# Moving GpSimd's second k*v of a pass to the end of the pass before, and the third of the first pass up to VectorE's bonus

## What is computed

```python
xn = _ln(x, ln1_w, ln1_b)
sx = _token_shift(xn, state[:, i1])
xxx = tanh((xn + sx * maa_x) @ maa_w1) ... @ maa_w2
x5 = xn[:, :, None] + sx[:, :, None] * (maa_stack + xxx)
w = exp(-exp(time_decay + tanh(x5[:, :, 1] @ decay_w1) @ decay_w2))
r, k, v = x5[:, :, 3] @ Wr.T, x5[:, :, 0] @ Wk.T, x5[:, :, 2] @ Wv.T
g = silu(x5[:, :, 4] @ Wg.T)
def step(s, rkvw):
    a = k_t[:, :, :, None] * v_t[:, :, None, :]
    out = einsum('bhk,bhkd->bhd', r_t, u * a + s)
    return (a + w_t[:, :, :, None] * s, out)
...
x = x + (group_norm(att) * g) @ Wo.T
...
x = x + rr * (kk @ ffn_Wv.T)
```

## Time and profile before

| | us |
|---|---|
| median of three runs | 703.38 (702.08 to 706.02) |
| the profiled execution | 699.89 |
| its span in the profile | 698.0 |
| TensorE busy | 623.4 (89%) |
| VectorE busy | 595.5 (85%) |
| ScalarE busy | 390.9 (56%) |
| GpSimd busy | 294.3 (42%) |

### The profile page before, as it was taken

How to read it: one execution, slowest core, us unless ns; L and a number is a source line. 1 busy time by engine, 2 the same in 40 slices (tenths; PEclk the granted TensorE clock), 3 DMA queues, 4 the chain that set the end, 5 groups by cost and what they waited for, 6 DMA issues and landing times.

```text
span 698.0 us, 9609 instructions
## 1 busy us (share of the span) xinstructions
PE 623.4 (89%) x2694; PEld 335.1 (48%) x2694; DVE 595.5 (85%) x902; ACT 390.9 (56%) x933; POOL 294.3 (42%) x210
## 2 busy tenths in 40 slices
PE   8999999979787859899899989989988998987887
PEld 5666666656332223354445435344543534444366
DVE  2999999974578998989997997999799799889853
ACT  3888888843443255476375555737546564353252
POOL 1111363001125283566629437564841945590020
PEclk9999999999999879999999999999999999998799
DMA  2433221202361542367266145616706540670020
GB/s 67 119 121 108 79 72 58 90 5 31 103 138 28 109 91 45 57 129 147 31 132 142 28 87 133 110 30 150 150 1 126 132 73 12 138 150 31 0 31 30
DMA packets 42445, 57.87 MB, mean 83 GB/s; under 512 B 4979, under 2 KB 25107, under 8 KB 42419
## 3 DMA queue, kind: packets, MB, share of 16 engines
q1 hardware_dynamic: 33008, 46.77, 29.3%
q0 software_dynamic: 9104, 10.77, 8.6%
q10 hardware_dynamic: 306, 0.02, 0.0%
HBM read 16.13 MB, written 7.86 MB: 34 GB/s over the span
## 4 chain that ended last, share of the span: by engine, by line
PE 26%; DVE 19%; issue 14%; POOL 7%; ACT 2%; DMA 1%; SPq 1%; DVEq 0%; POOLq 0%; ACTq 0%
DVE state L1455 9%; PE ps_c L874 7%; PE ps_a L789 6%; POOL state L656 3%; PE ps_c L789 3%; DVE vb L1460 2%; PE ps_att L854 2%; POOL x L680 2%; PE ps_a L812 2%; PE ps_a L817 2%; POOL xn L646 1%; DVE x L1415 1%; DVE sx L1533 1%; DVE bonus L1426 1%; DMA vb<-v 1%
## 5 line engine op out<-in xcount | busy, mean ns | idle before, releaser
L680 POOL TENSOR_TENSOR x<-x,xn 128x1024 f32<-128x1024 f32 x35 | 86.2, 2472 | 157.6 <-DVE x L1415 157.6
L1455 DVE TENSOR_TENSOR_SCAN state<-ps_w,state 128x512 f32<-128x512 f32 x128 | 145.8, 1199 | 0.2
L789 PE MATMUL ps_a<-x,wsq 128*128 128x512 f32 x256 | 122.1, 621 | 9.1 <-POOL x L680 6.5
L656 POOL TENSOR_TENSOR state<-vb,k 128x2016 f32<-128x2016 f32 x23 | 109.0, 4740 | 21.7 <-DMA vb<-v 10.6
L1460 DVE TENSOR_TENSOR vb<-state,r 128x2048 f32<-128x2048 f32 x32 | 104.9, 3278 | 1.7
L789 PEld LDWEIGHTS ps_a<-x,wsq 128*128 128x128 f32 x256 | 49.8, 200 | 69.9 <-issue 62.2
L1415 DVE SCALAR_TENSOR_TENSOR x<-ps_a,vec,sx 128x512 f32<-128x512 f32 x80 | 56.2, 745 | 26.3 <-PE ps_a L812 14.2
L310 ACT ACTIVATE probs<-ps_f,negmax 128x256 f32<-128x256 f32 x128 | 58.9, 472 | 1.6 <-DVE negmax L364 0.9
L812 PE MATMUL ps_a<-mix_t,w 64*128 64x512 f32 x128 | 49.6, 642 | 7.6 <-ACT mix_t L1157 5.2
L854 PE MATMUL ps_att<-vb,pick 128*32 128x512 f32 x256 | 36.5, 644 | 11.0 <-DVE vb L1460 11.0
L1113 ACT ACTIVATE zn<-wyz,rs 128x256 f32 (+1 forms) x60 | 31.1, 594 | 24.1 <-POOL rs L640 24.1
(11 more groups left out here) (213 smaller groups left out, 1271.1 us busy)
## 6 DMA issues: line engine op xcount, KB each, us to landing
vb<-v SPq DMA_DIRECT2D x120, 256.0 KB, 5.5
x<-in_x SPq DMA_DIRECT2D x32, 128.0 KB, 2.1
c<-in_ctx SPq DMA_DIRECT2D x32, 128.0 KB, 2.2
wyz<-in_x POOLq DMA_DIRECT2D x7, 512.0 KB, 5.8
out<-wyz SPq DMA_DIRECT2D x7, 512.0 KB, 7.5
out<-sx POOLq DMA_DIRECT2D x7, 512.0 KB, 9.3
vb<-v SPq DMA_DIRECT2D x16, 128.0 KB, 2.4
wsq<-in_wsq POOLq DMA_DIRECT2D x7, 256.0 KB, 3.4
```

Of the source, the lines that this page charges most:

```text
L656: nc.gpsimd.tensor_tensor(st[q][:, :, :, 1:L], src[:, :, :, 0:L - 1], wide(k[p][h][:, :])[:, :, :, 0:L - 1], ALU.mult).then_inc(kv_at(n, h ...
L680: nc.gpsimd.tensor_tensor(x5[j % 2][:, :, :], x5[j % 2][:, :, :], xn[:, :, 1:L1], ALU.add).then_inc(x5_ready, 1)
L789: mm = nc.tensor.matmul(bank[:, :], wsq[:, weight, c, P * o:P * o + P], src(c), start=(c == 0), stop=(c == EC - 1))
L1455: nc.vector.tensor_tensor_scan(row, w[h][:, :], row, 0.0, ALU.mult, ALU.add).then_inc(scanned, 1)
```

## The change

On GpSimd, and only there, k*v (n,0,1) moves from the head of pass n to the end of the pass before, behind add_x(n,4) and (in `body`) ahead of add_out. For chunk 0 it stands at the end of `fill_pass`. In `first_pass`, k*v (0,1,0) moves up ahead of add_x(1,0), behind a new wait `hold` for both of VectorE's bonuses. No instruction with work is added or taken away, and the order of the k*v among themselves stays.

```diff
+            def hold(n):
+                pool.wait_ge(bonus_ready, n * 2 + 2)
...
             def fill_pass(n, p):
                 q = 1 - p
                 prev(n + 1, sx_ready, xprev, t["prev1"], xn)
                 z_add(n + 2)
                 rstd(n + 2, ln1_var, ln1_rstd, ve1, rs1)
+                b_kv(n + 1, q, 0, 1)
 
             def first_pass(n, p):
                 q = 1 - p
                 prev(n + 1, sx_ready, xprev, t["prev1"], xn)
-                b_kv(n, p, 0, 1)
+                hold(n)
+                b_kv(n, p, 1, 0)
                 add_x(n + 1, 0)
                 add_x(n + 1, 1)
                 z_add(n + 2)
-                b_kv(n, p, 1, 0)
                 add_x(n + 1, 2)
                 add_x(n + 1, 3)
                 b_kv(n + 1, q, 0, 0)
                 add_x(n + 1, 4)
                 rstd(n + 2, ln1_var, ln1_rstd, ve1, rs1)
+                b_kv(n + 1, q, 0, 1)
 
             def body(n, p, z=True):
                 q = 1 - p
                 prev(n - 1, sx2_ready, xprev2, t["prev0"], xn2)
-                b_kv(n, p, 0, 1)
                 prev(n + 1, sx_ready, xprev, t["prev1"], xn)
...
                 b_kv(n + 1, q, 0, 0)
                 add_x(n + 1, 4)
+                b_kv(n + 1, q, 0, 1)
                 add_out(n - 1)
 
             def last_pass(n, p):
                 q = 1 - p
-                b_kv(n, p, 0, 1)
                 prev(n - 1, sx2_ready, xprev2, t["prev0"], xn2)
                 b_kv(n, p, 1, 0)
```

## The result

The changed kernel took 691.27 us (median of 4 runs, 689.89 to 694.57) beside 702.73 us for the kernel before (4 runs, 700.88 to 706.02): a ratio of 0.9855, 95% interval 0.9817 to 0.9893. Faster, as forecast, but by 11.5 us where 6.6 were forecast; the 696.8 us and the range from 693.0 us were too high.

The account below looks back on a forecast made before the run. The prediction had TensorE, ScalarE and VectorE arriving almost together at c_gn and a_mod in a steady pass. Gains of 4.1 (first pass), 1.5 (steady) and 1.0 us (last) made 6.6, so 703.38 became 696.8 us, range 693.0 to 701.5.

Parts of the forecast that it names:

- The mechanism: VectorE's product stands still while GpSimd's k*v runs; moved under the scans, the k*v no longer meets it, 2.15 us a pass.
- The steady passes: Passes 2 to 6: 0.3 us each of VectorE's 2.15, limited by ScalarE's Exp ahead of c_gn; 1.5 us in all.
- The first rival: Steady passes gain all of TensorE's 0.84 us gap instead of 0.3; 9.3 us in all, 694.1 us, chance 0.12.
- The copies behind the product: Steady pass: four small GpSimd copies done by 505.4 us, leaving a_shift, which needed 505.48 before, 0.1 us in hand.
- a sign of being wrong: Steady pass: a_shift released by the copies with c_gn late would show the forecast wrong.
- The last pass: Product ends 1.47 us sooner, c_gn then held by Exp; 1.0 us gained, bounds 0 and 1.47.
- The collision of b_ruk: Last pass: k*v (7,1,0) still runs between b_ruk's two operations, 5.74 us instead of 1.4, only 1.47 us sooner.
- The first pass: Second product, blocked for 7.15 us, ends 4.86 us sooner; 4.1 us of it kept, bounds 3.0 (or 2) and 4.86.
- that full clock: First pass: TensorE's sums of the second product, without the gap before them, take half of 1.94 us.
- three terms: First pass 4.1 us, steady passes 1.5 us, last pass 1.0 us; sum 6.6 us.
- the third rival: TensorE's low clock lasts through the front of pass 1, doubling some 15 us of work; 5.4 us slower, 708.8 us, chance 0.08.
- the yardstick: The 703.38 us median of three runs of the kernel before, from which the 6.6 us were taken.

Follow-up runs that it names:

- no_hold: The changed kernel without the wait for the bonuses ahead of k*v (0,1,0) in the first pass; 699.1 us, ratio 0.996 to the kernel before.
- last_early: The changed kernel with its last pass reordered on VectorE and ScalarE, scans, product and VectorE's k*v earlier; 692.25 us, ratio 0.9867 to the kernel before.
- act_dose: The changed kernel with one more ScalarE copy between group norm's Ln and Exp; 696.02 us, ratio 0.9916 to the kernel before.
- steady_only: The kernel before with only k*v (n,0,1) moved to the end of the pass before; 697.5 us, ratio 0.995.
- the controls: The changed kernel with no edit, measured once in each of three series; 691.78, 692.6 and 692.36 us, ratios 0.989, 0.9888 and 0.9875 to the kernel before.
- before_warm: The kernel before with 20 matmuls on constants in four TensorE gaps of the first pass, no k*v moved; 697.71 us, ratio 0.9949.
- first_only: The kernel before with only the hold and k*v (0,1,0) moved up in the first pass; 698.16 us, ratio 0.9962.
- again3: The changed kernel with no edit, measured again in the third series; 692.36 us, ratio 0.9875 to the kernel before.
- after_warm: The changed kernel with 14 matmuls on constants in the first pass and 20 in the last; 693.41 us, ratio 0.9888 to the kernel before.

## Why the forecast was right and where it failed

**Right, with its size.**
- The mechanism: a product and a k*v don't run side by side, and the k*v put under the scans is out of the way. The Trainium skill's page "SBUF — State Buffer", section "Who interferes with whom", gives it as an exclusive lock between GpSimd's reads and a VectorE operation with two SBUF inputs, and the traces agree: 7.15 us for 2.29 before the change, 5.60 for 1.41 in no_hold, 3.00 for 1.03 in last_early, and 1.19 to 1.22 us for the scans, one of whose inputs is in PSUM, whatever stood beside them.
- The steady passes: 0.3 us each forecast, 0.26 to 0.33 found, in four of the five (1.15 us for 1.5). Pass 6 gave none: I had taken it for a repeat of pass 5 without reading its Exp. That ScalarE is the bound was tested by act_dose. The first rival, the whole 0.84 us of TensorE's gap, is out.
- The copies behind the product: the forecast gave them 0.1 us in hand and named an a_shift released by them as a sign of being wrong. It is released by them, 0.28 us late, but that costs nothing: c_gn waits for the Exp, and starts 0.15 us sooner behind the product, where 0.14 was worked out.
- The last pass: 1.0 us forecast, 0.97 found at c_gn. The collision of b_ruk, which was to stay, went; with Exp as the bound, this wrong term changed nothing, which is luck. The gain at the last product is 0.40 us.
- The first pass: 4.1 us forecast, 4.57 found, of which 1.7 us is the full clock on matmuls that ran at half before, and the block itself 2.9. The forecast took in that full clock without a reason other than the missing gap; steady_only had it with the gap in place. The sums took 1.07 us for 1.94, as taken, and followed the matmuls ahead of them without a gap; the spread of v started at 229.59 where 230.4 was forecast, 0.4 us of it the earlier start of the whole.

The forecast's three terms then make 6.7 us where 6.6 were forecast.

**The step that failed** is the one on TensorE's clock. The forecast used it once as a gain, "without the gap that came before I take the full clock, half of 1.94", and otherwise only as the third rival, on the slower side: "If the low level (1.2 for 2.4 GHz) then lasts through the front of pass 1". There was no case in which the clock gives more back than that. Yet the same trace had the clock at 0.50 over 256 to 264 us, right behind the block that the change shortens. I knew it (the third rival says that "3 do so now") and priced it only as something that could get worse. A blocked product costs its own 2 to 5 us, then the gap that it makes on TensorE, and at times the matmuls behind the gap at half the clock. The sum lacked a term for the third in the front of pass 1, the last pass and the drain, 2.9 us net in the two profiles (0.64 us of it a chance stretch in pass 3). That such a term is real and of 2 to 3 us: the controls' gain of 8.5 to 9.3 us lies 1.9 to 2.7 over the forecast; before_warm gains 3.4 us with the long products in place; no_hold loses 3.1 of its 7.3 us to it; the median of the mean clocks goes from 0.968 to 0.980. That it is tied to each block is not shown: steady_only's clock stayed full behind one.

The Trainium skill's page "TensorE: Matmul & The Clock Gate", section "HAM oscillation — how this bites in real kernels", says of a kernel with long waits between its bursts of matmuls that each next burst starts on the lower level. The rows with the longest waits agree: 3.78 us for 1.99 behind 3.74 us of waiting in no_hold, and 1.06 us for a pair that takes 0.59 behind 3.55 us in the last pass. Behind the shorter wait of the first pass they go both ways: 2.00 us behind 1.74 us before, 1.12 us behind 1.73 us in steady_only.

**The second part of the miss** is the yardstick. The forecast added its 6.6 us to a median of 703.38 us; the kernel before then stood at 702.73, 700.67, 701.07, 701.65 and 701.38 us in five comparisons. Their mean is 701.5 us, 1.9 us under the yardstick. With the controls' 8.5 to 9.3 us of gain the changed kernel stands at 691.8 to 692.6 us, still under the range, which had no room for the clock on that side.

**What stays open.** Some of the clock's gain is the same in every execution profiled: from the first product to pass 1's second, the four profiles of the changed kernel take 70.28 to 70.38 us and first_only 70.32; the drain is told above. Some is not: a steady pass has now and then a stretch of half clock worth 0.6 to 0.8 us (pass 3 before, pass 2 in again3 and steady_only, passes 2 and 4 in first_only), and again3's last product came 39.7 us behind the last pass's first where the other three show 38.6. There is one profile of the kernel before, so its 76.10 us in front, and with them the split of the clock's gain, hold for that execution; that the clock gives some 2 to 3 us beyond the forecast is what the runs together show. Why first_only and steady_only together fall 3 us short of the whole change is not explained: the clocks say that TensorE's level has a part in it, single executions have another, and no run separated them. What makes the level fall behind a wait in one run and not behind the same wait in another isn't shown either.

## What to carry to other kernels

Keep GpSimd's operations that read SBUF away from VectorE's operations with two inputs in SBUF, under those that have one in PSUM. Small ones count as much as large ones: in the profile, rstd on 128 x 4 elements under a product undid a whole reordering, and one wait in the right place, the hold here or the one on rstd, brought it back. When a block is removed, price the gap that it makes on TensorE too, by reading the granted clock of the stretches behind it, and price a low level found there as something that may be won as well as lost; when gaps are filled by hand, look where the low level goes next.

## What the runs showed of the hardware that was not expected

- The same wait on TensorE is followed by the half level in one execution and not in another: 1.74 us before, 1.73 in steady_only.
- The lock holds for a SCALAR_TENSOR_TENSOR (b_ruk) as for a TENSOR_TENSOR: 5.60 us for a pair that takes 1.41.
- It works the other way for a few elements too: 3.00 + 1.26 us for GpSimd's two operations on 128x4, 1.03 + 0.20 us alone.
- GpSimd's DMA issues were not lengthened: add_out took 1.33 us from 492.05 over the start of a product (492.76), for 1.34 before, and z_add took 1.28 us from 513.45, all of it under a product (511.97 to 515.66).
- Filling matmuls on constants can pay for themselves: 20 of them gained 3.4 us in before_warm. 20 in the last pass, in after_warm, gained nothing.
